# Four experts' second products in one group, with eight slots for their inner values

## What is computed

```python
x = x + conv(ln(x))     # deformable 3x3 sampling, 8 groups of 8 channels, bilinear corners,
                        # offsets and softmax masks from a depthwise conv + norm + gelu
t = tokens(x)
t = t + ffn(ln(t))      # 8 experts, two used by each token

# the ffn of the reference
logits = xt @ Wr + br;  probs = softmax(logits);  top_p, top_idx = top_k(probs, 2)
xe = xn[None] * ln_g[:, None] + ln_b[:, None]
h = gelu(einsum('end,edh->enh', xe, W1) + b1[:, None])     # 64 -> 256 for each of 8 experts
y = einsum('enh,ehd->end', h, W2) + b2[:, None]            # 256 -> 64
out = (weights * y[top_idx]).sum()
```

## Time and profile before

| | |
|---|---|
| median of 3 runs | 331.36 us (327.48, 331.36, 331.92) |
| the profiled execution's own time | 327.07 us |
| its span, first to last instruction | 325.3 us |
| mean granted TensorE clock | 0.982 |

### The profile page before, as it was taken

How to read it: one execution, slowest core, us unless ns; L and a number is a source line. 1 busy time by engine, 2 the same in 40 slices (tenths; PEclk the granted TensorE clock), 3 DMA queues, 4 the chain that set the end, 5 groups by cost and what they waited for, 6 DMA issues and landing times.

```text
span 325.3 us, 8588 instructions
## 1 busy us (share of the span) xinstructions
PE 284.0 (87%) x3369; PEld 186.0 (57%) x3369; DVE 243.7 (75%) x715; ACT 260.0 (80%) x484; POOL 107.5 (33%) x111
## 2 busy tenths in 40 slices
PE   8778798856899989989999799989979999987894
PEld 3543465633567765566667665665646556654462
DVE  5899968999958999896588988893656724456735
ACT  2663978879797899999978799999869988862863
POOL 5032323503442604063437050352533406164000
PEclk9799799999799999999999999999999999999998
DMA  7310000000000000000000000000000000000000
GB/s 156 99 32 0 2 4 3 1 2 0 2 3 2 4 2 0 2 2 8 3 11 2 2 2 2 1 11 0 10 2 2 2 1 2 10 0 11 0 2 17
DMA packets 5638, 3.39 MB, mean 10 GB/s; under 512 B 5073, under 2 KB 5278, under 8 KB 5534
## 3 DMA queue, kind: packets, MB, share of 16 engines
q1 hardware_dynamic: 5598, 2.84, 3.9%
HBM read 2.04 MB, written 0.52 MB: 8 GB/s over the span
## 4 chain that ended last, share of the span: by engine, by line
PE 37%; DVE 30%; ACT 20%; issue 9%; POOL 4%; POOLq 0%; DVEq 0%; ACTq 0%
ACT wk L1172 6%; PE m_ps L1468 6%; ACT wk L1167 5%; DVE prod L780 5%; PE zl_ps L1376 4%; PE zh_ps L1373 4%; PE m_ps L1451 3%; PE ga_ps L1391 3%; PE m_ps L1453 3%; PE ga_ps L1393 2%; PE ga_ps L1392 2%; ACT h_all L1194 2%; PE ga_ps L1434 2%; DVE w_low L818 2%; POOL y_r L482 2%
## 5 line engine op out<-in xcount | busy, mean ns | idle before, releaser
L1167 ACT ACTIVATE wk<-zh_ps 128x512 f16<-128x512 f32 x144 | 86.7, 602 | 25.6 <-PE zh_ps L1373 23.7
L780 DVE TENSOR_TENSOR prod<-ga_ps,wx 128x480 f32<-128x480 f32 x96 | 61.9, 652 | 42.3 <-PE ga_ps L1393 40.6
L1172 ACT ACTIVATE wk<-zl_ps 128x512 f16<-128x512 f32 x144 | 86.7, 602 | 0.1
L1391 PE MATMUL ga_ps<-v_all,wk 128*128 128x80 f16 x576 | 76.7, 203 | 7.6 <-DVE prod L780 6.7
L489 POOL TENSOR_TENSOR prod<-prod 128x960 f32<-128x960 f32 x16 | 35.6, 2228 | 138.7 <-DVE prod L780 138.7
L1392 PE MATMUL ga_ps<-v_all,wk 128*128 128x80 f16 x576 | 76.6, 203 | 0.0
L1393 PE MATMUL ga_ps<-v_all,wk 128*128 128x80 f16 x576 | 76.6, 203 | 0.0
L1391 PEld LDWEIGHTS ga_ps<-v_all,wk 128*128 128x128 f16 x576 | 57.1, 99 | 18.8 <-issue 8.2
L1392 PEld LDWEIGHTS ga_ps<-v_all,wk 128*128 128x128 f16 x576 | 57.7, 100 | 8.3 <-issue 0.5
L1373 PE MATMUL zh_ps<-tab,sel_hi 128*128 128x512 f16 x144 | 55.7, 387 | 6.5 <-ACT wk L1167 4.8
L1376 PE MATMUL zl_ps<-tab,sel_lo 128*128 128x512 f16 x144 | 56.2, 390 | 4.6
(11 more groups left out here) (269 smaller groups left out, 510.2 us busy)
## 6 DMA issues: line engine op xcount, KB each, us to landing
h_all<-in_W SPq DMA_DIRECT2D x1, 512.0 KB
w_s<-in_W SPq DMA_DIRECT2D x1, 512.0 KB
x_tok<-in_x SPq DMA_DIRECT2D x1, 384.0 KB, 4.1
out_dram<-x_tok SPq DMA_DIRECT2D x6, 64.0 KB, 2.2
w_high<-w_high SPq DMA_DIRECT2D x1, 256.0 KB, 2.8
const<-in_table SPq DMA_DIRECT2D x1, 218.0 KB, 3.0
vec<-in_vectors SPq DMA_DIRECT2D x1, 132.5 KB
x_tok<-in_x SPq DMA_DIRECT2D x1, 128.0 KB, 2.3
```

What stands on the lines that cost most here:

```text
L780: dve.tensor_tensor(prod[q % 2][:].rearrange("p k n -> p (k n)")[:, f * PB * NV:(f + 1) * PB * NV] .rearrange("p (n c l) -> p n c l", n=PB ...
L1167: act.activation(wk[n % WR][:, 0, :], zh_ps[:], ACT.Relu, scale=W_SCALE).then_inc(s_wkh, 1)
L1172: act.activation(wk[n % WR][:, 1, :], zl_ps[:], ACT.Relu, scale=W_SCALE).then_inc(s_wkl, 1)
L1391: pe.matmul(to, w_h, high, start=True, stop=False)
```

## The change

The slots for inner values go from four to eight (HR), so h_all takes twice the SBUF; `w1_raw`, which shares its place for the loading of W1, is bound to the first four slots as before. The table times of `expert_out` become equal in pairs, each being the time of the later one (27 and 28 become 28 and 28), so that two calls of `expert_out` stand next to each other in TensorE's order. ScalarE's, VectorE's and GpSimd's orders aren't touched. PE_FIRST has new values too, but the first body has no experts. The tail doesn't use the tables for `expert_out`; there the only difference is the number of slots.

```diff
-HR = 4
+HR = 8
 ...
 PE_MIDDLE = {...
-             "expert_out": [17.5, 19, 20.5, 23, 27, 28, 30.5, 32.5], "outputs_t": [25.5, 35.5], "b2": 35.5}
+             "expert_out": [19, 19, 23, 23, 28, 28, 32.5, 32.5], "outputs_t": [25.5, 35.5], "b2": 35.5}
 PE_LAST = {...
-           "expert_out": [17.5, 18.5, 20.5, 23, 26.5, 27, 31.5, 32], "outputs_t": [25, 34.5], "b2": 23}
+           "expert_out": [18.5, 18.5, 23, 23, 27, 27, 32, 32], "outputs_t": [25, 34.5], "b2": 23}
 ...
         h_all = sb("h_all", [P, HR, HC, 2 * P])
         h_t = [h_all[:, r, :, :] for r in range(HR)]
-        w1_raw = h_all[0:C, :, :, :].rearrange("p r a n -> p (r a n)")
+        w1_raw = h_all[0:C, 0:E * HID // (HC * 2 * P), :, :].rearrange("p r a n -> p (r a n)")
```

More of the change, by code:

```diff
@@ L54 @@
             "expert_in": [6, 12.5, 12.5, 14.5, 15.5, 21, 25, 27, 31.5, 34.5, 34.5, 34.5, 34.5, 34.5, 34.5, 34.5],
-            "expert_out": [11.5, 14, 15, 18.5, 20.5, 23, 25.5, 26], "outputs_t": [25, 35], "b2": 25}
+            "expert_out": [14, 14, 18.5, 18.5, 23, 23, 26, 26], "outputs_t": [25, 35], "b2": 25}
 ACT_FIRST = {"pad_image": 2.5, "project_high": 6.5, "image_out": 9.5, "conv_gelu": 14.5, "tap_exp": 21.5, "hat_x": 25.5,
```

## The result

The changed kernel has a median of 333.55 us (329.08 to 335.61, 20 runs), the kernel before 330.74 us (325.16 to 334.10, 20 runs) in the same comparison. The ratio is 1.0125, 95% interval 1.0078 to 1.0171. A second comparison on another chip gave 1.0076 (1.0036 to 1.0117). The change makes the kernel slower by about one per cent, less than the 2% that were set as the bound. The ratios leave out executions that are over 1.5% above the fastest of their kernel, so they aren't the quotients of the medians, and the profiled execution of the changed kernel is one of those left out.

What follows compares the result with a forecast made beforehand. ScalarE was taken to bound bodies 1 and 2, TensorE more body 3, each handing the other one bank at a time. 2.1 us (bodies 1 and 2) + 0.45 (body 3) = 2.55; 329.46 + 2.55 = 332.0 us, range 326.0 to 336.5.

Steps and rivals of the forecast that it cites:

- The price of a group: TensorE, in and out of half-width form: single group 1.02 us, second joined one 0.87, each pair saves 0.24 us.
- The waits of `expert_out` and the slots: The 1.9 us of waits for yb, and those for es, vanish; more slots for `hidden` free nobody, term 0.
- Step 1: Body 1, times 17.5 to 19: table load covers the pair, product 0.87 us later, taken as +0.1 us.
- Step 2: Body 1, time 20.5: the removed group's 0.29 us ScalarE wait goes; together with 17.5 to 19: 0, at best -0.3.
- Step 3: Body 1, time 23: third eviction waits for the pair's end, next `weights_high` starts +0.71 us later.
- Step 4: Body 1, times 27 and 28: ScalarE has `hat_x` anyway, vanished 0.96 us wait worth nearly nothing, lag +0.5 us.
- Step 5: Body 1, time 30.5: the removed group gives ScalarE back 0.3 us, lag +0.22 us.
- Step 6: Body 1, time 32.5: third eviction waits for the pair, `weights_high` +1.05 us late, nothing behind takes it back.
- Body 3: Third body: +0.87 us at 18.5, 0.73 us wait given back at 20.5, later lags; sum +0.45 us.
- Full counting of TensorE's time: Rival: every switch of form lies on the path, 4.8 us gained with the waits, 322.3 us; chance 0.17.
- Covered at both ends: Rival: third eviction finds its products ready, lags sum to about nothing, 327.1 us; chance 0.18.
- Starved everywhere: Rival: 0.87 us lag stays at each of 12 pairs, 10.4 us slower, 337.5 us; chance 0.10.

Runs made afterwards that it cites:

- the pair at 28 alone: Eight slots, only m = 4 and 5 joined, at 28 (27 in body 3), all others single, against the kernel before: 329.98 us, ratio 1.0020.
- the later evictions: Changed kernel with ScalarE's output evictions moved from 23.5 and 32.5 to 24 and 33: 341.77 us, ratio 1.0261 to the kernel before.
- the last pair elsewhere: Changed kernel with the last pair of bodies 1 and 2 at 32, body 3's last groups apart: 332.75 us, ratio 1.0102 to the kernel before.

## Why the prediction was right, and where it was off

The direction and the size came out, and so did the mechanism in body 1: 2.55 us were forecast, 2.9 us are in the traces, 2.8 +- 0.4 in the times at equal clock. The median forecast was 332.0 us and 333.55 were measured; 1.3 us of this lies in the kernel before, whose median was taken as 329.46 and came out at 330.74.

*The price of a group.* Taken as 0.87 us for a second one, 0.86 measured; 0.24 us saved, 0.25 measured.

*The waits of `expert_out` and the slots.* Both as said: the waits for yb and es vanish, no step of `hidden` was freed, slots alone give 0.00.

*Step 1,* +0.1 at unit 20 for ScalarE: 0.12. *Step 2,* back where it was: +0.05 at unit 22. *Step 3,* +0.71 with a third eviction waiting: +0.58, waiting 0.54. *Step 4,* +0.5 behind `hat_x`, the vanished wait worth nearly nothing: +0.37, and the pair at 28 alone is worth 0.18. *Step 5,* +0.22: ScalarE's `weights_high` of unit 31 starts 157.88 - 4.54 = 153.34, +0.11. *Step 6,* +1.05: 0.95, and 0.88 at the last unit.

*Body 3,* +0.45 up to its last unit: +0.37. At 18.5 the lag was +0.87 as forecast, and the missing group at 20.5 gave it back to -0.24 at unit 21. The path was partly another one: the third eviction was to wait about 0.7 and 0.9 us in this body too, and waits 0 and 0.21 us; the lag at unit 24 was +0.99 and not +0.7.

*What failed* is what I put at nothing for VectorE and what stands behind it, in two places, by 0.8 us in all. The first is that body 2 repeats body 1 because it has the same tables. VectorE's `weigh` comes 1.2 us later there, in the kernel before too, so at the pair at 28 TensorE waits for VectorE and not only for ScalarE. That gives away 0.15 us with the pair at 28 alone (-0.03 against -0.18), and 0.37 us in the changed kernel (1.25 against 0.88), where the pair at 23 has made VectorE later still and the wait is 0.86 us. VectorE's 5.5 us free in the stretch of body 1 said nothing of this place. The second is the tail, where GpSimd's tree and everything behind it keep 0.4 us that the main loop had won back. I had asked who waits on ScalarE's queue for the pair and hadn't followed VectorE's and GpSimd's to their ends. That the sum came so near is in part luck: the lags taken in body 1 were each about 0.1 us too long, and with body 3's 0.08 us this hid 0.4 us of it in the sum.

*The rivals.* Full counting of TensorE's time is refuted by the pair at 28 (0.18 us gained out of 1.2 in body 1, 0.03 in body 2) and by the changed kernel itself. Covered at both ends is refuted by the third eviction's waits. Starved everywhere is refuted by unit 22 and unit 29 of body 1, where the lag is back near 0.

*The time.* I had put it between the two places in which the runs seemed to fall. With 68 runs there are no two places but a spread with the granted clock, from a mean of 327.13 us (20 runs with a clock of 0.98) to 331.13 us (21 runs at 0.96). In the 0.98 group the changed kernel has 330.45 us (10 runs).

*Open.* The first comparison's 4.1 us (1.25% of about 330) and the second's 2.5 us lie on both sides of 2.9. Whether the change also makes the half-clock stretch of body 3 more likely isn't settled. It is at the same unit in both profiles of the changed kernel and in that of the later evictions (254.9 us), and in none of the eight others, though all of them have the 1.69 us wait in front of it. The mean clocks over all runs, 0.9686 changed and 0.9708 before, differ by 0.5 us' worth.

## What to carry to other kernels

Where two engines hand one buffer to and fro, as here, saved time on one of them is worth what the other one's queue lets through: ask of each place what the partner has in hand while the joined work runs (here a table load or a long activation: nearly free; four evictions, two of which need the result of that very work: not free). Then ask the same of every other engine whose results the place needs, and in each loop body by itself: two bodies with the same tables differed by 1.2 us in when VectorE came to the same unit. A wait that is named in the profile can be the smaller of two that end together; moving the waiting instruction away made this kernel 7 us slower. Subtracting the start times of a recurring instruction in two profiles found tenths of a microsecond here that the medians of twenty runs don't show.

## What the runs showed of the hardware

With the clock full, the schedule repeats between chips to 0.02 us over stretches of 40 us (0.88 and 0.89, 1.25 and 1.26, 0.37 and 0.38). Most of the spread between runs of one kernel goes with the granted clock: of the 2.2 us of scatter among the 68 runs of before, 1.0 us is left about the line on the clock. The clock is lost in stretches of 3.4 us (or two or four of them) at 1.2 instead of 2.4 GHz, each worth 0.8 to 1.6 us where it could be read off the lags (0.81 and 0.95 us in the two profiles of the changed kernel, 1.58 us in that with the last pair elsewhere). They lie mostly in the start-up, at about 85 us and at the very end, and in some profiles also in the middle of the kernel.

One VectorE instruction of one shape and type (L759, 128x288 fp32) takes 0.46 us in body 1 and 1.23 us in body 2, to 0.01 us in the profiles of before and after; no run isolates why.
